# A four-block network on one core: the quantised network's first rows normalised inside the attention ahead of it, and bias terms ordered anew

## The reference, cut to what matters

```python
x = x + jnp.tanh(g_xattn[0]) * _L0_xattn_ref(_layernorm(x, axis=-1), ctx_1024, mask_Bx1xSxS2_ff0, L0_xattn_wq, L0_xattn_wk, L0_xattn_wv, L0_xattn_wo)
x = x + jnp.tanh(g_ffn[0]) * _L0_ffn_ref(_layernorm(x, axis=-1), L0_ffn_qweights, L0_ffn_scales, L0_ffn_biases, L0_ffn_lora_a, L0_ffn_lora_b, L0_ffn_ln_gamma, L0_ffn_ln_beta)
x = x + jnp.tanh(g_xattn[1]) * _L1_xattn_ref(_layernorm(x, axis=-1), ctx_1024, fside_BxSxS2_0, ...
```

## Time and profile before

| what | value |
|---|---|
| median of 3 runs | 3192.49 us (3189.13 to 3194.62) |
| the profiled execution's own time | 3189.76 us |
| its span | 3188.5 us |
| PE, DVE, ACT, POOL busy | 95%, 66%, 38%, 27% of the span |
| mean granted PE clock | 0.984 |

### The profile page before, as it was taken

The page is one execution under the profiler, slowest core; times in us unless marked ns, Lnnn a source line. Parts: engine busy times, 40 slices in busy tenths (PEclk is TensorE's granted clock), DMA queues, the critical chain, the costliest instruction groups (busy, mean ns, idle before and its releaser), DMA issues.

```text
span 3188.5 us, 43629 instructions
## 1 busy us (share of the span) xinstructions
PE 3015.9 (95%) x16384; PEld 2215.5 (69%) x16384; DVE 2119.3 (66%) x3869; ACT 1225.8 (38%) x2357; POOL 860.7 (27%) x1302
## 2 busy tenths in 40 slices
PE   7999999999999999999999999899998888997996
PEld 5778877667767776777689999666666754555664
DVE  6996879567855885587378897784218777764113
ACT  5443332553355235432233333341224346662331
POOL 2206400100110010001156556450343231112554
PEclk9999999999999999999999999999999999998998
DMA  7000100010001000200032222003551011113533
GB/s 189 18 1 1 30 27 1 14 43 27 1 14 56 14 1 14 68 1 1 1 93 80 83 91 67 21 1 106 188 189 37 21 41 46 35 38 115 209 125 109
DMA packets 104614, 176.42 MB, mean 55 GB/s; under 512 B 27125, under 2 KB 75799, under 8 KB 99671
## 3 DMA queue, kind: packets, MB, share of 16 engines
q1 hardware_dynamic: 89527, 102.32, 10.4%
q0 software_dynamic: 14880, 71.33, 6.3%
HBM read 198.31 MB, written 17.56 MB: 68 GB/s over the span
## 4 chain that ended last, share of the span: by engine, by line
PE 76%; DVE 15%; issue 4%; ACT 2%; POOL 2%; DMA 1%; SPq 0%; DVEq 0%; ACTq 0%; POOLq 0%
PE psum L424 8%; PE psum L447 8%; PE psum L1438 7%; PE psum L2572 6%; PE psum L1450 6%; PE psum L1919 5%; PE psum L1874 5%; PE psum L2593 3%; PE psum L414 2%; PE psum L1159 2%; PE psum L460 2%; PE psum L762 2%; PE psum L2748 2%; PE psum L3173 2%; DVE psum L3431 1%
## 5 line engine op out<-in xcount | busy, mean ns | idle before, releaser
L424 PE MATMUL psum<-Vt,shared 128*128 128x256 f32 (+1 forms) x1600 | 362.7, 382 | 0.4
L447 PE MATMUL psum<-Kt,xnTt 128*128 128x512 f32 (+1 forms) x960 | 346.2, 511 | 4.0 <-ACT xnTt L537 4.0
L424 PEld LDWEIGHTS psum<-Vt,shared 128*128 128x128 f32 (+1 forms) x1600 | 298.5, 191 | 39.6 <-issue 1.2
L447 PEld LDWEIGHTS psum<-Kt,xnTt 128*128 128x128 f32 x960 | 180.9, 191 | 162.9 <-issue 158.9
L245 POOL TENSOR_SCALAR root_v<-meanvar 128x8 f32<-128x8 f32 (+3 forms) x19 | 8.6, 455 | 903.7 <-DVE meanvar L223 903.7
L1450 PEld LDWEIGHTS psum<-expert_w,prep 128*128 128x128 f32 x1024 | 194.6, 190 | 77.7 <-issue 57.4
L1450 PE MATMUL psum<-expert_w,prep 128*128 128x256 f32 x1024 | 240.8, 379 | 0.0
L1438 PE MATMUL psum<-weights,expert_w 128*128 128x512 f32 x512 | 240.3, 593 | 0.0
L3431 DVE CUSTOM_DVE_ANT_0 psum<-psum,expert_w 128x128 f32<-128x128 f32 (+7 forms) x256 | 191.6, 776 | 72.6 <-PE psum L3173 69.3
L1364 DVE SCALAR_TENSOR_TENSOR bias<-Kt,small,bias 128x1232 f32<-128x1232 f32 x96 | 149.2, 1554 | 129.7 <-ACT Kt L1348 128.4
L3320 ACT ACTIVATE prep<-psum 128x512 f32<-128x512 f32 (+3 forms) x384 | 167.0, 493 | 104.7 <-PE psum L3196 103.8
(11 more groups left out here) (516 smaller groups left out, 6699.8 us busy)
## 6 DMA issues: line engine op xcount, KB each, us to landing
weights<-in_L_ffn_w SPq DMA_DIRECT2D x32, 512.0 KB, 4.7
expert_w<-in_L_ffn_w SPq DMA_DIRECT2D x32, 512.0 KB, 4.6
expert_w<-in_L_xattn_Wf SPq DMA_DIRECT2D x16, 512.0 KB, 5.8
weights<-q_parts SPq DMA_DIRECT2D x32, 144.0 KB
weights<-k_parts SPq DMA_DIRECT2D x96, 48.0 KB
weights<-in_L_xattn_Wk SPq DMA_DIRECT2D x4, 1024.0 KB, 4.9
weights<-in_L_xattn_Wv SPq DMA_DIRECT2D x4, 1024.0 KB, 7.0
weights<-in_L_xattn_Wq SPq DMA_DIRECT2D x4, 1024.0 KB, 5.4
```

The costliest lines, as they stand in the source:

```text
L424: ins = pe.matmul(o_bank(t), probT[0:rows, t % 2, c, :], Vt[0:rows, t // TB, c, :], start=(c == 8), stop=(c == 7))
L447: ins = pe.matmul(flat[:, par * 3 * BANK + at:par * 3 * BANK + at + cols], xnTt[:, par, k, :], Kt[:, t // TB, k, src:src + cols], start=(k ...
```

## The change

It has three parts.

1. In the first preparation VectorE takes the statistics of all 16 tiles in a row and aggregates at once, and its hinges come behind. ScalarE holds one hinge back at the first value, makes none at the last two, and makes four behind `keep_tile(0)` and `keep_tile(1)`, where it had two ahead of them. `first_bias` moves to `prep`, the hinge buffers to the end of `inner`.
2. The statistics of tiles 0 to 5 are aggregated in tile 8 of the attention, and pairs 0, 1 and 2 normalised in its tiles 11, 12 and 13. Turns 0 and 1 of the quantised loop stand in the last tile on TensorE and ScalarE, turn 0 on VectorE behind `residual(14)`. The 26 products go. Tiles 6 to 15 are aggregated behind the last hinge, have a root of their own on GpSimd, and are normalised in VectorE's turns 1, 2 and 3.
3. In the attention of the third block `turn_tile(t + 3)` stands behind `of_pair(t)`.

```diff
--- before.py
+++ after.py
@@ -570,6 +570,8 @@ (act_wide, behind the ten values)
             keep_tile(0)
             keep_tile(1)
+            if between:
+                between(4 * NTE + VT_USES)
@@ -680,6 +682,8 @@ (dve_wide)
             if t >= 1:
                 residual(t - 1)
+        if tail:
+            tail()
         residual(NT - 1)
@@ -811,10 +815,10 @@ (pe_attention)
             if feed:
                 if t + 2 < NT:
                     scores(t + 2)
+                if t < NT - 1:
+                    of_pair(t)
                 if t + 3 < NT:
                     turn_tile(t + 3)
-                if t < NT - 1:
-                    of_pair(t)
@@ -1128,8 +1132,9 @@
-    first_bias = flat_rows[:, 0:NT * S2]
-    first_hinge = flat_rows[:, NT * S2:3 * NT * S2].rearrange("p (n c) -> p n c", n=2)
+    first_bias = prep[:, 2 * D:2 * D + NT * S2]
+    first_hinge = flat_rows[:, NT * D - 2 * NT * S2:].rearrange("p (n c) -> p n c", n=2)
+    EARLY = 3
@@ -1160,8 +1165,7 @@ (pe_quantised, act_quantised: now with a first and a last turn)
-        pe_stay_at_work(pe, bank_of(0, 0), 26)
-        for i in range(EVENTS + LAG_G + 1):
+        for i in range(first, last):
@@ -1207,19 +1209,16 @@
-    def dve_quantised(dve):
+    def dve_quantised_rows(dve, pair):
+        for t in range(2 * pair, 2 * pair + 2):
+            ins = normalise(dve, inner[:, t, :], x, t)
+        ins.then_inc(h_ready, 1)
+
+    def dve_quantised(dve, first, end):
...
-        dve_aggregate(dve)
-        dve_root(dve)
-        dve.wait_ge(w_made, NL)
-        for t in range(NT):
-            ins = normalise(dve, inner[:, t, :], x, t)
-            if t % 2:
-                ins.then_inc(h_ready, 1)
-        dve.wait_ge(rows_of_bias_landed, 16)
-        for i in range(EVENTS + LAG_G + 1):
+        for i in range(first, end):
@@ -1251,6 +1250,11 @@ (behind the scaling of turn i - 1)
+            if i == 1:
+                dve_root(dve, None, 2 * EARLY, NT)
+            if 1 <= i < 4:
+                for pair in range(EARLY + 2 * (i - 1), min(EARLY + 2 * i, PAIRS)):
+                    dve_quantised_rows(dve, pair)
@@ -1259,7 +1263,7 @@ (pool_quantised)
-        pool_root(pool, 1e-5)
+        pool_root(pool, 1e-5, 0, 2 * EARLY)
@@ -1269,6 +1273,8 @@
                 pool_root(pool, 1e-5, t, t + 2)
+            if i == 1:
+                pool_root(pool, 1e-5, 2 * EARLY, NT)
@@ -3632,8 +3638,9 @@ (pe_program)
-        pe_wide(pe, 0, None, True, None)
-        pe_quantised(pe)
+        pe_wide(pe, 0, None, True, lambda: pe_quantised(pe, 0, 2))
+        pe_quantised(pe, 2, EVENTS + LAG_G + 1)
@@ -3645,11 +3652,12 @@ (act_program)
-            for _ in range({NTE - 1: 3, 4 * NTE - 1: 2, 4 * NTE + VT_USES - 1: 2}.get(n, n >= 4 * NTE)):
+            for _ in range({NTE - 1: 3, 4 * NTE - 1: 2, 4 * NTE + VT_USES: 4}.get(n, 4 * NTE < n < 4 * NTE + VT_USES - 2)):
                 act_first_hinge(act, next(hinges))
...
-        act_wide(act, 0, 1, True, None, between, lambda t: [act_first_hinge(act, j) for j in [next(hinges, None)] if j is not None])
-        act_quantised(act)
+        act_wide(act, 0, 1, True, lambda: act_quantised(act, 0, 2), between, lambda t: [act_first_hinge(act, j) for j in [next(hinges, None)] if j is not None])
+        act_quantised(act, 2, EVENTS + LAG_G)
@@ -3671,15 +3679,12 @@ (dve_program)
             dve.bn_stats(bn6[:, t, :], x[:, t, :]).then_inc(dve_step, 1)
             vs()
-            if t >= 7 and t % 2:
-                dve_first_hinge(dve, next(hinges))
-            if t in (9, 13):
-                dve_lora(dve, 2 + t // 13)
         dve_aggregate(dve)
-        for j in range(4, NL):
+        for j in range(2, NL):
             dve_first_hinge(dve, next(hinges))
             dve_first_hinge(dve, next(hinges))
             dve_lora(dve, j)
+        dve_first_hinge(dve, next(hinges))
         dve.wait_ge(tanh_made, 1)
@@ -3691,11 +3696,23 @@ (one_more(t), once in each tile of the attention)
+            if t == 8:
+                dve_aggregate(dve, 0, 2 * EARLY)
+            elif t == 10:
+                dve_root(dve, None, 0, 2 * EARLY)
+                dve.wait_ge(w_made, NL)
+            elif 11 <= t < 11 + EARLY:
+                dve_quantised_rows(dve, t - 11)
+
+        def first_event():
+            dve.wait_ge(rows_of_bias_landed, 16)
+            dve_quantised(dve, 0, 1)
...
-        dve_wide(dve, 0, x, tanh_g[:, 0:1], one_more)
+        dve_wide(dve, 0, x, tanh_g[:, 0:1], one_more, first_event)
         for j in hinges:
             dve_first_hinge(dve, j)
-        dve_quantised(dve)
+        dve_aggregate(dve, 2 * EARLY, NT)
+        dve_quantised(dve, 1, EVENTS + LAG_G + 1)
```

More of the change, by code:

```diff
@@ L652, in dve_softmax, with dve_wide @@
         dve.tensor_tensor(Pb, Pb, total.unsqueeze(2).to_broadcast([P, H, S2]), ALU.mult).then_inc(weights_made, 1)
-    def dve_wide(dve, n, stream, gate, between):
+    def dve_wide(dve, n, stream, gate, between, tail=None):
         g0 = NT * n
@@ L1147, in sp_quantised, with pe_quantised @@
         sp.dma_start(brow, a["L0_ffn_biases"].rearrange("(o j) d -> o j d", o=1).to_broadcast([P, NL, D])).then_inc(rows_of_bias_landed, 16)
-    def pe_quantised(pe):
+    def pe_quantised(pe, first, last):
         def turn_pair(src, dst):
@@ L1189, in pe_quantised, with act_quantised @@
                 multiply_pair(gT[:, m % 2], 2 * (m // PAIRS) + 1, bank_of(3, m)).then_inc(h_product, 1)
-        pe.wait_ge(h_ready, PAIRS + EVENTS)
-    def act_quantised(act):
-        act.wait_ge(quants_landed, 16 * 11)
-        for i in range(EVENTS + LAG_G):
+    def act_quantised(act, first, last):
+        for i in range(first, last):
             if i < EVENTS:
@@ L3634, in pe_program @@
         pe_setup(pe)
-        pe_wide(pe, 0, None, True, None)
-        pe_quantised(pe)
+        pe_wide(pe, 0, None, True, lambda: pe_quantised(pe, 0, 2))
+        pe_quantised(pe, 2, EVENTS + LAG_G + 1)
+        pe.wait_ge(h_ready, PAIRS + EVENTS)
         pe_decoder(pe)
@@ L3647, in between @@
         def between(n):
-            for _ in range({NTE - 1: 3, 4 * NTE - 1: 2, 4 * NTE + VT_USES - 1: 2}.get(n, n >= 4 * NTE)):
+            for _ in range({NTE - 1: 3, 4 * NTE - 1: 2, 4 * NTE + VT_USES: 4}.get(n, 4 * NTE < n < 4 * NTE + VT_USES - 2)):
                 act_first_hinge(act, next(hinges))
-        act_wide(act, 0, 1, True, None, between, lambda t: [act_first_hinge(act, j) for j in [next(hinges, None)] if j is not None])
-        act_quantised(act)
+        act_wide(act, 0, 1, True, lambda: act_quantised(act, 0, 2), between, lambda t: [act_first_hinge(act, j) for j in [next(hinges, None)] if j is not None])
+        act.wait_ge(quants_landed, 16 * 11)
+        act_quantised(act, 2, EVENTS + LAG_G)
         act_decoder(act)
```

## The result

| | before | after |
|---|---|---|
| median of 5 runs | 3192.49 us (3186.12 to 3195.53) | 3175.79 us (3169.65 to 3179.92) |
| profiled execution, span | 3189.76, 3188.5 | 3179.92, 3178.6 |
| mean granted PE clock | 0.984 | 0.983 |

The ratio is 0.9953, with a 95% interval of 0.994 to 0.9967. The forecast was 3176.5 (3169 to 3184). The profiled execution of after is the slowest of its five, so its time says less than the starts of single instructions in its trace. The medians of before in this and the three later groups, 3192.49, 3191.64, 3192.0 and 3190.47 us, lie 2.0 us apart.

What follows compares the result with a forecast made beforehand. VectorE set the first attention's pace; the network's end hung on when its second product stream began. Terms -4.7 + 3.0 - 2.4 - 9.1 - 1.5 = -14.7 us gave 3175.1 to 3177.8, taken as 3176.5, range 3169 to 3184.

Steps and rivals of the forecast that it cites:

- The first preparation: Ahead of the first attention: ScalarE's copies precede its hinges, first softmax near 64.6 for 69.3; -4.7 us, bounds 2.5 and 7.
- Added to the tiles: First attention's tiles: six aggregates and six rows on a full VectorE cost +3.0 us, 5.4 if each row meets GpSimd.
- The last tile: First attention's last tile: new work fills TensorE's idle 4.01 us and keeps its upper clock; -2.4 us, bounds 0 to 2.5.
- The start: Quantised network: second product stream begins 15.6 us behind the first attention's end, not 25.6; -9.1 us, bounds 6 and 11.
- The attention of the third block: Third block: products first fill TensorE's wait for VectorE's row, gain limited by VectorE's score waits; -1.5 us, bounds 0 and 4.7.
- The late rows block the start: Rival, chance 0.15: at the network's start late rows meet GpSimd's operations; start gains 6, sum 11.6, total 3180 us.
- Part of the gain is not there: Rival, chance 0.13: first softmax gains 2.5, last tile 0 or third block's attention 0; with all three 8.6, 3183 us.
- Slower: Rival, chance 0.03: in the third block the later row turn delays ScalarE's copy, up to 23.6 us, total 3200.
- nothing measurable: Rival, chance 0.05: TensorE's full stretch starts about 20 us behind the first attention; total gain under 6.4 us, 3187.

Runs made afterwards that it cites:

- prep_only: The kernel before with only the first preparation changed (part 1, hinge buffers moved too): 3184.90 us, ratio 0.998.
- latent_kept_before: The kernel before with 13 more unused products ahead of the last step's heads and two behind each of four later score products: 3192.89 us, ratio 1.0005.
- boundary_only: The kernel before with only the passage from first attention to quantised network changed (part 2, buffers moved too): 3190.25 us, ratio 0.9995.
- boundary_again: The kernel before with only part 2 of the change, run once more for a second trace and set of medians: 3188.33 us, ratio 0.9986.
- gap_products: The changed kernel with 24 unused products in TensorE's wait ahead of turn 3 of the quantised network: 3173.86 us, ratio 0.9941.
- attention_only: The kernel before with only the turn of the rows put behind `of_pair` in the third block's attention (part 3): 3188.88 us, ratio 0.9991.
- early_root: The changed kernel with last hinge, aggregate and root of tiles 6 to 13 ahead of tile 15's residual, separate root for tiles 14 and 15: 3172.85 us.

## Why the prediction was right

**The first preparation** (-4.7): after's first softmax is 6.1 us earlier than before's. But before's trace has the latest of six such starts (66.86 to 69.32 in the traces without part 1), and behind the first tiles the distance has settled: the fifth tile's softmax starts at 108.54 instead of 114.44, 5.9 earlier. `prep_only` gave 6.7 in the medians. The mechanism was the one named. What I had mis-sized is the scores' clock: they take 8.51 us in after for 10.88 before, the case that I had put in the bound. That belongs to the change: they take 8.51 in all eight traces with part 1 and 10.34 to 11.19 in all six without.

**Added to the tiles** (+3.0): the sixteenth softmax starts 3.5 us earlier than before's, from 5.9 at the fifth, so 2.4. A tile with two rows took 10.64 for 9.99; they cost 0.65 and not 0.82.

**The last tile** (-2.4): E is 5.4 earlier, from 3.5, so 1.9. The clock came back in full (1.31 + 4.51); TensorE's turns began 0.5 later, because the softmax's last operation took 1.99 for 1.44 while GpSimd's addition for the first pairs ran beside it. The 2.4 itself was this one trace's. From the sixteenth softmax to E before took 17.0 us, but the other four traces without part 2 took 16.2 and 16.3, and all nine with it 15.2. Against those four the term is 1.1 and not 1.9: there the last tile's turns and products lost 1.6 us to the lower clock, not 2.4.

**The start** (25.6 to 15.6 behind E, less 0.7 for a wait, taken as -9.1): 15.4, so -10.2 for the stream's start. Four traces without part 2 beside before's have E + 24.8 to 27.0, the changed kernel's two others E + 15.7 and 15.9, so this size holds. The wait of 0.7 did not come: TensorE's only waits for scaled rows are two at the network's end, of 1.63 and 2.21 us, and before has the same two (1.66 and 2.21). What after's trace has besides is 1.6 us lost at that end, because the final products ran at half clock, 5.25 for 3.62. In after:

```profile
342.69 6.12 POOL L354 MEMSET prep<- 128x7232 f32 x1
342.79 6.49 DVE L267 TENSOR_SCALAR Vt<-Vt,meanvar,rstd 128x256 f32<-128x256 f32 x2
342.94 4.18 PE L379 MATMUL psum<-ident 128*128 128x128 f32 x36
...
349.33 0.75 PE L1158 MATMUL psum<-ident,Vt 128*128 128x128 f32 x4 [2.21 <-DVE Vt L267]
349.88 5.25 PE L1164 MATMUL psum<-expert_w,shared 128*128 128x256 f32 x16
```

and in before and in `latent_kept_before`, which has before's code there:

```profile
365.52 3.62 PE L1159 MATMUL psum<-expert_w,shared 128*128 128x256 f32 x16
```

```profile
365.82 5.31 PE L1159 MATMUL psum<-expert_w,shared 128*128 128x256 f32 x16
```

So this loss is not shown to be the change's. Six of the fourteen traces have it (4.86 to 5.31 us), one of them with before's code, and `boundary_only`, `boundary_again` and `gap_products` take 3.62.

These five terms give -5.9 + 2.4 - 1.9 - 10.2 + 1.6 = -14.0, the mark at (a) for this pair of traces; the forecast's four gave -13.2.

**The attention of the third block** (-1.5): 2.5 over its tiles. VectorE's bias additions of the sixth and the sixteenth tile, first in before and then in after:

```profile
2061.32 1.44 DVE L948 TENSOR_TENSOR shared<-psum,bias 128x1232 f32<-128x1232 f32 x1 [0.80 <-PE psum L762]
...
2124.30 1.44 DVE L948 TENSOR_TENSOR shared<-psum,bias 128x1232 f32<-128x1232 f32 x1
```

```profile
2046.97 1.44 DVE L952 TENSOR_TENSOR shared<-psum,bias 128x1232 f32<-128x1232 f32 x1 [0.80 <-PE psum L766]
...
2107.45 1.43 DVE L952 TENSOR_TENSOR shared<-psum,bias 128x1232 f32<-128x1232 f32 x1
```

That is 60.5 for 63.0 us, and `attention_only` and `prep_only` give the same 60.5 and 63.0. I had taken VectorE's waits for scores, 1.9 us, as the most that could be had. The waits behaved: between these two additions VectorE's idle time fell from 2.2 to 0.8 us, which is the 1.5 of the forecast. The bound failed because VectorE's busy time fell too, from 60.7 to 59.7: four of its eleven normalising rows (line 267) took 0.9 us instead of 0.4 beside a GpSimd operation, where in before it was five, which is 0.5 of this 1.0. Where the other half comes from is open. The middle of my wide bound (0 to 4.7) was right.

**The rivals.** *The late rows block the start* is half there: the first four late rows took 2.30 us beside GpSimd's addition, and the next four, without one, 1.38. The forecast had put 0.4 us for one such addition into its E + 8.0, and it cost 0.9: pair 3 is turned at E + 8.4. It cost no more, since the scaling of these events met no addition (0.70 each). The Trainium skill ("SBUF — State Buffer", Who interferes with whom) says that the second to issue of a GpSimd instruction and a `tensor_scalar` in a two-port mode waits for the whole of the other; for the addition the trace agrees: the first row began 0.08 us behind its start, took 1.33 us for 0.40 and ended 0.15 us behind its end. All 17 rows of line 267 in after that began with over 0.4 us of such a wide GpSimd operation (256 columns or more) still to run ended 0.15 us behind it. For the power the trace does not agree, and the further 2 us that the rival took from it were not there to lose:

```profile
250.29 0.85 POOL L250 TENSOR_TENSOR rstd<-root_v,minus_half 128x2 f32<-128x2 f32 x1
```

```profile
250.36 1.38 DVE L267 TENSOR_SCALAR inner<-x,meanvar,rstd 128x256 f32<-128x256 f32 x4
```

The first of these rows began 0.07 us behind the power and took 0.41. Of the eight rows in after that began with over 0.4 us of a power to run none took more. Whether that is the operation or its 2 to 10 columns no run here separates.

*Part of the gain is not there* came in none of its three parts: the first softmax, the last tile's clock and the attention all gained. *Slower* and *nothing measurable* did not come. For *slower* ScalarE's copy of the row would have had to come late: TensorE's scores wait 0.2 us in all for a copy in after's 2000 to 2150 us.

**What stays open.** By marks the changed kernel is 16.0 to 19.5 us ahead at (b), by medians 14.5 to 16.7, and most of the difference hangs on part 2: 9.4 to 9.8 at (a), 7.5 at (b), and 1.4 and 3.7 in two sets of medians. 1.7 of it is shown, the fall of the clock after the decoder's gap, in all three traces of part 2 alone and in none of the other eleven; why this gap costs it there was not found. The rest is lost in the last 700 us, where the clock falls at one place or another in every trace, before's too, and no run shows whether part 2 has a share in that. That the sum of my terms (14.7) met the median is therefore partly luck. The marks had gained 2.6 more at (b), and the late stages took it back. And the terms missed in both directions: the preparation, the tiles, the start and the third block's attention gave 1.2, 0.6, 1.1 and 1.0 us more than I had put, the last tile 0.5 less, and 1.6 went at the network's end.

## What to carry to other kernels

Fill the wait in front of the last tile with the first work of the next stage, and look at once at what the next wait hangs on: here a chain of hinge, aggregate and root, of which all but two columns could be moved ahead too, for another 4.6 us. When unused products go, see where the next gap is: 24 of them there were worth 1.6 us at the stream's start, and nothing more once the gap itself was halved. A price read from one trace can be that trace's alone: the last tile's clock was worth 2.4 us in the trace of before and 1.6 in four others. Compare marks stage by stage before medians, and medians before single traces, since a gain early in a long kernel can be smaller at its end.

## What the runs showed of the hardware

- A VectorE `tensor_scalar` row of 128x256 that began beside a wide GpSimd operation ended 0.15 us behind it, in after 17 times of 17. A `memset` of 6.12 us, which only writes, did it too: the row that began 0.10 us behind its start took 6.17 us for 0.40, in before and in after.
- A power of 2 to 10 columns on GpSimd held no such row: eight in after began with over 0.4 us of one to run, and none took more than 0.41 us.
- A two-input VectorE operation and GpSimd hinder each other in both directions: the softmax's `tensor_tensor` took 1.99 for 1.44 beside GpSimd's addition, and a GpSimd multiplication of two columns 1.29 for 0.20 beside a hinge in `early_root`.
- After the same gap of 0.64 us, at the same instructions, the clock fell in three traces of part 2 alone and in none of the other eleven, and shifting it by 4.56 us did not change that.
- Near 2555 us the clock fell in six traces of eleven, for up to 7 us between (b) and (c), with the same instructions around it; none of the three traces with 13 and 8 more unused products has it, which five of the eleven haven't either.
- The same final products of the quantised network took 3.62 us in eight traces and 4.86 to 5.31 in six, and a trace of before's code is among each.
